# Layer 0 of a four-layer graph network: the reciprocal inside the decay is computed on ScalarE (ln, then exp) where it was computed on VectorE

## The reference, cut to what matters

```python
decay_raw = jnp.tanh(jax.nn.relu(dec_in @ Wd1 + bd1) @ Wd2 + bd2)
decay = jnp.exp(decay_scale[None, :] * decay_raw)
euclid = euclid * decay
...
hyp = -hyp_beta[None, :] * man_dist * decay
logits = alpha * euclid + (1.0 - alpha) * hyp
```

## Time and profile before

| what | us |
|---|---|
| median of 3 runs (4308.51 to 4311.9) | 4309.06 |
| profiled execution, its own time | 4316.74 |
| span of its trace | 4315.0 |
| DVE busy in the span | 3413.9 (79%) |
| PE busy | 3231.9 (75%) |
| ACT busy | 2173.5 (50%) |

### The profile page before, as it was taken

How to read it: one execution, slowest core, us unless ns; L and a number is a source line. 1 busy time by engine, 2 the same in 40 slices (tenths; PEclk the granted TensorE clock), 3 DMA queues, 4 the chain that set the end, 5 groups by cost and what they waited for, 6 DMA issues and landing times.

```text
span 4315.0 us, 86344 instructions
## 1 busy us (share of the span) xinstructions
PE 3231.9 (75%) x31243; PEld 2713.9 (63%) x31243; DVE 3413.9 (79%) x6840; ACT 2173.5 (50%) x6347; POOL 1715.7 (40%) x2078
## 2 busy tenths in 40 slices
PE   1388888788888532566646788858799999779995
PEld 1155566556665321566645677745799999779995
DVE  5499999789999544999967878767666666779997
ACT  2366777667777222788844576630322222234443
POOL 0356677566666310000002200000455555458883
PEclk7699999999999666787877899979899999989998
DMA  4778888888888201000002211123344444213332
GB/s 91 229 221 244 241 267 265 212 242 258 259 261 259 91 15 40 8 12 11 11 10 93 80 40 41 46 94 123 112 126 125 124 128 123 89 65 128 127 129 67
DMA packets 306659, 550.64 MB, mean 128 GB/s; under 512 B 80311, under 2 KB 207993, under 8 KB 306089
## 3 DMA queue, kind: packets, MB, share of 16 engines
q1 hardware_dynamic: 252073, 380.67, 28.4%
q0 software_dynamic: 54144, 164.25, 13.6%
HBM read 433.68 MB, written 111.07 MB: 126 GB/s over the span
## 4 chain that ended last, share of the span: by engine, by line
PE 43%; DVE 37%; ACT 7%; issue 7%; DMA 3%; SPq 2%; POOL 1%; DVEq 0%; ACTq 0%; POOLq 0%
PE psum L3763 5%; PE psum L2490 4%; PE psum L3779 4%; PE psum L3714 4%; PE psum L3712 4%; DVE arena_a L1917 3%; PE psum L3679 2%; PE psum L3066 2%; PE psum L3738 2%; ACT arena_c L3029 2%; DVE arena_a L1913 2%; DVE arena_c L1925 2%; DVE arena_a L3259 2%; PE psum L2518 2%; PE psum L3351 2%
## 5 line engine op out<-in xcount | busy, mean ns | idle before, releaser
L1224 POOL DMA_INDIRECT arena_a<-src_table,src_tix x808 | 809.3, 1002 | 563.6 <-issue 387.0
L3483 POOL TENSOR_SCALAR node_hot<-arena_c 128x128 fp32r<-128x128 f32 x575 | 368.5, 652 | 902.0 <-DVE arena_c L3371 568.6
L3501 DVE SCALAR_TENSOR_TENSOR msg_parts<-psum,msg_parts 128x512 fp32r<-128x512 f32 (+2 forms) x644 | 425.6, 661 | 259.6 <-ACT msg_parts L3650 227.7
L3650 ACT ACTIVATE msg_parts<-psum 128x512 fp32r<-128x512 f32 (+2 forms) x325 | 186.4, 574 | 520.4 <-PE psum L3714 520.4
L3201 POOL TENSOR_SCALAR node_hot_dst<-arena_c 128x128 fp32r<-128x128 f32 x587 | 383.3, 670 | 122.9 <-DVE arena_c L3605 67.9
L3066 PE MATMUL psum<-arena_a,arena_c 128*128 128x150 f32 x1800 | 288.8, 330 | 174.0 <-ACT arena_c L3032 174.0
L3712 PE MATMUL psum<-arena_c,arena_a 128*128 128x128 bf16 x3675 | 406.4, 220 | 0.0
L3714 PE MATMUL psum<-arena_c,arena_a 128*128 128x128 bf16 x3675 | 406.4, 220 | 0.0
L3066 PEld LDWEIGHTS psum<-arena_a,arena_c 128*128 128x128 f32 x1800 | 283.2, 224 | 177.1 <-ACT arena_c L3032 177.1
L1408 ACT ACTIVATE arena_a<-arena_a 128x128 f32<-128x128 f32 x808 | 239.8, 298 | 254.3 <-DVE arena_a L1915 253.8
L3191 POOL TENSOR_SCALAR arena_a<-arena_a,arena_c 128x2500 bf16<-128x2500 bf16 x8 | 60.9, 7611 | 709.2 <-DMA arena_a<-bucket_lists 709.2
(11 more groups left out here) (609 smaller groups left out, 9841.2 us busy)
## 6 DMA issues: line engine op xcount, KB each, us to landing
y_rows<-arena_c SPq DMA_DIRECT2D x101, 576.0 KB, 4.1
arena_a<-bucket_rows SPq DMA_DIRECT2D x150, 384.0 KB
arena_c<-near_keys SPq DMA_DIRECT2D x101, 256.0 KB, 5.6
arena_b<-near_keys SPq DMA_DIRECT2D x101, 252.0 KB
arena_a<-bucket_rows SPq DMA_DIRECT2D x50, 448.0 KB
arena_a<-bucket_lists SPq DMA_DIRECT2D x25, 896.0 KB
pair_counts<-arena_c SPq DMA_DIRECT2D x25, 800.0 KB
arena_a<-bucket_lists SPq DMA_DIRECT2D x25, 704.0 KB
```

The lines of the kernel that those rows point to most:

```text
L1224: e.indirect_dma_start(out_, None, table, bass.IndirectOffsetOnAxis(ap=idx, axis=0)).then_inc(sem, 16)
L3483: return e.tensor_scalar(node_hot[at % RING_M][:, i, :], iota_row, src_lo[:, b, 2 * k + j:2 * k + j + 1], None, ALU.is_equal)
L3501: e.scalar_tensor_tensor(out=to[:, 1, 0:nt, :], in0=bank[at % 4][:, 0:nt * P].rearrange("p (t f) -> p t f", f=P), scalar=0.0, in1=to[:, 0, ...
```

## The change

The two DVE instructions are gone. ACT gets two new ones in place on the same tile: Ln with 1 added to its input, and Exp with the sign turned, so exp(-ln(1 + x)) = 1/(1 + x). The Ln stands ahead of the first half of the squares, the Exp behind the relu of the hidden layer. The semaphore `decay_inverse` now counts two steps a block, so the last exp waits for 2 * i1 + 2.

```diff
                 if b1:
+                    e.wait_ge(g.decay_exp, i1 + 1)
+                    e.activation(tlog[s1][:, 3, :], tlog[s1][:, 3, :], ACT.Ln, bias=1.0).then_inc(g.decay_inverse, 1)
                     act_w_squares(e, i1, 0)
...
                     e.activation(hid_2[s0], bank[0][:, :], ACT.Relu).then_inc(g.hid_act, 1)
+                if b1:
+                    e.wait_ge(g.decay_inverse, 2 * i1 + 1)
+                    e.activation(tlog[s1][:, 3, :], tlog[s1][:, 3, :], ACT.Exp, scale=-1.0).then_inc(g.decay_inverse, 1)
                 if b2:
                     e.wait_ge(g.less_ready, i2 + 1)
                     e.activation(tlog[s2][:, 2, :], tlog[s2][:, 0, :], ACT.Exp).then_inc(g.exp_rows, 1)
...
                 if b1:
-                    e.wait_ge(g.decay_inverse, i1 + 1)
+                    e.wait_ge(g.decay_inverse, 2 * i1 + 2)
...
                     dve_l0_messages(e, i3)
-                if b1:
-                    e.wait_ge(g.decay_exp, i1 + 1)
-                    own.step(e.tensor_scalar(tlog[s1][:, 3, :], tlog[s1][:, 3, :], 1.0, None, ALU.add))
-                    e.reciprocal(tlog[s1][:, 3, :], tlog[s1][:, 3, :]).then_inc(g.decay_inverse, 1)
```

## The result

The changed kernel takes 4302.99 us (median of 20 runs, 4300.22 to 4306.67), the kernel before, beside it, 4311.74 us (20 runs, 4305.09 to 4317.48). The ratio is 0.9979 with a 95% interval of 0.9973 to 0.9986. By the medians the changed kernel is 8.75 us faster. The profiled execution has a span of 4300.5 us.

A forecast was written before the change was run, and what follows sets the result against it. The prediction took DVE as the bound in the first stretch, elsewhere a ring of PE and ACT with a leg over DVE. Terms of -16.6, +3.3, +4.5, +0.7 and +0.6 gave -7.5 us from 4309.06, so 4301 us, range 4287 to 4317.

The forecast's parts named there:

- A ring of PE and ACT with a leg over DVE: Loop pass closes through PE and ACT, 11.69 or 11.68 us without the DVE leg, which ends slightly later than ACT's.
- the first stretch: 24 passes counting positions over 808 columns, 12.58 us each; second: 22 over 128 columns, 11.74; third: 45 without counting, 11.79.
- The removal is worth 0 in the second and third stretch: DVE's 1.12 us add and reciprocal lie outside its leg there; in the first stretch DVE's cycle falls to 11.46 us.
- The Ln is hidden: Ahead of the squares of half 0, it takes 0.30 to 0.40 us of ACT's idle time, nothing on the path.
- The Exp costs its step of 0.20 us: Between relu and exp on ACT, it adds 0.20 us, making the ring 11.89 us in every stretch.
- The slack of 0.10 and 0.06 us: ACT's leg ahead of the squares has 0.10 us to spare in the third stretch and 0.06 in the second.
- The sum: Stretches -16.6, +3.3 and +4.5 us, two intervals between them +0.7, six longer ones +0.6: together -7.5 us.
- The hidden Exp: Rival, chance 0.14: DVE's leg stays the later one, the Exp in ACT's leg costs nothing; -20 us, 4289 us.
- The dearer Exp: Rival, chance 0.15: the Exp in ACT's leg costs more than its neighbour; at a 0.40 us step, +12 us, 4321.
- The held first stretch: Rival, chance 0.08: something else holds the first stretch at 12.58 us; only losses remain, +8 us, 4317.
- The full gain: Rival, chance 0.05: DVE's busy time counts in full, 101 x -1.12 = -113 us, 4196 us.
- The boundary: For the whole kernel, 0.2% (8.6 us) separates change from none: 4300.4 or 4317.7 us; faster 0.44, within 0.41, slower 0.15.

The follow-up runs named there:

- without gathers: From the fifth block GpSimd writes 1.0 instead of gathering rows, on the fourth chip: kernel before 4323.85 us, changed kernel 4319.63 us.
- The removal by itself: Kernel before without DVE's add and reciprocal, nothing added on ACT, output not the reference's, on the second chip: ratio 0.9991 to the kernel before.
- the early Exp: Changed kernel with Exp moved directly behind Ln: 1.0000 and 1.0006 against the kernel before on two slow chips; 4305.16 us without gathers.
- one filler less: Two instead of three matmuls whose result nobody reads, on the early Exp: 4235.96 us without gathers; with them 0.9936, as on the kernel before.
- the additions alone: Kernel before, add and reciprocal kept on DVE, plus one Ln and one Exp on a spare tile on ACT: ratio 1.0004, on a third chip 1.0034.

## Why the prediction was right

The forecast was 4301 us from a sum of -7.5 us; measured were 4302.99 us and -8.75 us. The forecast stood on a median of 3 runs of the kernel before, 4309.06 us, and 20 runs gave 4311.74. So the base was 2.7 us too low and the sum 1.3 us too small, and the two in part cancel. By its steps:

- *A ring of PE and ACT with a leg over DVE, not DVE's busy time.* Shown: the pass follows the Exp's place and the number of fillers, and not DVE's load, except in the first stretch.
- *The removal is worth 0 in the second and third stretch, and brings the first down to the ring.* Shown without gathers, by the removal together with additions that lie in idle time: 11.75 for 11.74 there, 11.76 for 12.54 in the first. The removal by itself ran only at the slow pace.
- *The Ln is hidden.* It lies in ACT's idle time in the changed trace, and the early Exp puts both new instructions there with no loss over 0.01 us in the second and third stretch. Shown.
- *The Exp costs its step of 0.20 us.* The step is 0.20 us, and the ring went to 11.88 where I had 11.89. The slack of 0.10 and 0.06 us was read rightly too: the losses a pass are 0.09 and 0.14 us.
- *The sum.* With both kernels cut at starts of the last exp (the kernel before has 302.22, 258.36 and 530.42 us for 24, 22 and 45 passes then), the terms came out as -16.8 us over the 24 passes (-16.6 forecast), +3.0 over the 22 (+3.3) and +4.2 over the 45 (+4.5). Mis-sized was what lies between and ahead: I gave the eight other intervals +1.3 us, and they changed by less than 0.1 us together, while the first passes, which I left out, begin 1.0 us earlier and are 0.7 us shorter. That makes -11.5 us up to the last pass of the loop. Behind the loop the profiled executions differ by another -3.0 us, and nothing behind the loop changed. So the two profiled executions differ by -14.5 us where the medians differ by -8.75. The kernel before spreads over 12.4 us in its 20 runs, and its profiled one (4316.74) is among the slowest, so a sum over one pair of traces can't be told from the median to better than some 6 us: that -7.5 lies 1.3 us from the median is in part luck.
- *The rivals.* The hidden Exp (4289) is out for the Exp where the change puts it, and true for the Exp moved. The dearer Exp is out by its step. The held first stretch is out. The full gain is out.
- *The boundary.* I gave 0.44 to faster and 0.41 to the same. It came out at that boundary: 0.9979 is just beyond 0.998, and its interval (0.9973 to 0.9986) holds the boundary.

On the Trainium skill, page "ScalarE: Activation LUTs": the price without pointer operands (293 ns, a step of 200 ns by the section "What ACT_TABLE_LOAD costs") held for the durations of both new instructions (0.29 and 0.30 us) and for the step behind the Exp (0.20). Its advice to leave a reciprocal to VectorE (section "What it computes", which names accuracy as the reason) is about the function Reciprocal and not about time. The time here is 1.16 us on VectorE against 0.59 us for Ln and Exp on ScalarE; the kernel is faster by its first 25 passes, and slower in the other two stretches.

## What to carry to other kernels

Before you move work from the busiest engine, ask which of its instructions lie between the wait that PE ends and the signal that PE needs next. Here 1.12 us a pass lay outside that leg and were worth nothing in the 67 passes of the second and third stretch, while 0.20 us placed in the other leg cost 0.09 to 0.14. Two legs that end within 0.1 us of each other are one bound: read the slack of the second before you add to it, and put added work in front of a wait, not behind it. And when a microsecond doesn't pay, shorten the ring first: with one filler less the pass fell by 0.86 us without gathers, where DVE had been relieved, and the granted clock held at 1.00. And compare on one chip: at the pace of 17 to 20 us a pass the same edits were worth something else.

## What the runs showed of the hardware

One program differs by 13 to 15% between chips: the kernel before took 4311.74 us on the first chip and 4944.7, 4892.29 and 4893.71 us on three others. Nearly all of it lies in the loop with indirect gathers: from the first to the last start of the last exp, the traces of the kernel before and of the additions alone on the second chip have 1223.8 and 1827.6 us, 604 of the 627 us between their spans. The granted clock in the loop is 0.99 to 1.00 on the first chip and 0.76 to 0.80 on the second and third, the other two that were traced with gathers. Without the gathers the same kernel takes 4323.85 us on one of those three, with a granted clock of 1.00. And two activations of one kind, one behind the other, have starts 0.20 us apart though each is recorded as 0.30 us long, so the durations of a group overstate what an added ACT instruction costs.
